# A fused attention and feed-forward kernel: second copy of the gather indices, another setup, other places for late weight splits

## The reference

```
q, k, v = x Wq', x Wk', x Wv'          (32 query heads, 8 key heads, 128 wide)
q, k    = rope(rmsnorm(q)), rope(rmsnorm(k))
keys    = [512 cached keys read by page number, 128 new keys]
p       = softmax(q keys' / sqrt(128), cached keys beyond the length hidden)
c       = (p values) Wo'               (batch b reads 16 pages named by an index input)
s       = silu(c Wgate'), the smaller half of each row by magnitude set to 0
h       = s * (c Wup');  x1 = h Wdown' + x
y       = x1 weight[adapter of b]';  out = x1 + bias + (y W4')      (W4 unpacked from 4 bits)
```

## Time and profile before

| | us |
|---|---|
| three timed runs | 1416.01, 1419.3, 1423.49 |
| median | 1419.3 |
| profiled execution, device time | 1421.85 |
| its span, first to last instruction | 1419.8 |

### The profile page before, as it was taken

How to read it: one execution, slowest core, us unless ns; L and a number is a source line. 1 busy time by engine, 2 the same in 40 slices (tenths; PEclk the granted TensorE clock), 3 DMA queues, 4 the chain that set the end, 5 groups by cost and what they waited for, 6 DMA issues and landing times.

```text
span 1419.8 us, 22844 instructions
## 1 busy us (share of the span) xinstructions
PE 1374.2 (97%) x7750; PEld 1158.6 (82%) x7750; DVE 1186.1 (84%) x2596; ACT 876.2 (62%) x2228; POOL 786.7 (55%) x822
## 2 busy tenths in 40 slices
PE   5899999999999999999999999999999999999998
PEld 4788888888888888888878888888888777676766
DVE  7989898989898989898979898989899987666662
ACT  5667676767676767676757676767677752322221
POOL 6666666666666666666566656665766620222211
PEclk9999999999999999999999999999999999999999
DMA  6110211121111112111211121111121203121121
GB/s 222 60 31 27 75 61 34 34 72 60 30 58 48 60 31 75 32 61 33 71 30 60 33 73 33 62 33 66 37 71 31 102 19 117 48 73 45 45 62 51
DMA packets 26768, 80.41 MB, mean 57 GB/s; under 512 B 9523, under 2 KB 10547, under 8 KB 23187
## 3 DMA queue, kind: packets, MB, share of 16 engines
q1 hardware_dynamic: 10258, 45.29, 9.0%
q0 software_dynamic: 16384, 33.59, 8.1%
HBM read 76.74 MB, written 2.10 MB: 56 GB/s over the span
## 4 chain that ended last, share of the span: by engine, by line
PE 72%; POOL 9%; issue 7%; DVE 6%; DMA 4%; ACT 1%; SPq 0%; another core or an unknown queue 0%; POOLq 0%; DVEq 0%; ACTq 0%
PE proj_ps L108 7%; PE proj_ps L110 7%; PE turn_ps L715 7%; PE proj_ps L109 7%; PE out_ps L894 5%; PE value_ps L108 4%; POOL kg L515 4%; PE score_ps L110 4%; PE value_ps L109 4%; PE value_ps L110 4%; PE score_ps L108 4%; PE score_ps L109 3%; DMA vg<-vc,idx 3%; PE gu_ps L110 3%; PE gu_ps L108 3%
## 5 line engine op out<-in xcount | busy, mean ns | idle before, releaser
L515 POOL DMA_INDIRECT kg<-kc,idx x256 | 258.8, 1011 | 262.9 <-issue 257.0
L1129 ACT ACTIVATE probs<-probs,shift,rstd 128x640 f32<-128x640 f32 x256 | 234.4, 918 | 157.8 <-DVE shift L1441 154.0
L525 POOL DMA_INDIRECT vg<-vc,idx x256 | 258.6, 1010 | 71.4 <-issue 70.5
L1477 DVE TENSOR_TENSOR pt_lo<-turn_ps,pt_hi 128x512 fp32r<-128x512 f32 x320 | 217.4, 687 | 47.5 <-ACT pt_hi L1135 32.1
L1452 DVE CUSTOM_DVE_ANT_0 probs<-score_ps,mask 128x640 f32<-128x640 f32 x256 | 208.4, 820 | 42.6 <-PE score_ps L110 39.7
L1135 ACT ACTIVATE pt_hi<-turn_ps 128x512 fp32r<-128x512 f32 x320 | 186.7, 593 | 88.1 <-PE turn_ps L715 78.7
L108 PE MATMUL proj_ps<-w_hi,xt_hi 128*128 128x512 f32 (+1 forms) x512 | 196.3, 383 | 13.6 <-DVE w_lo L1373 9.7
L715 PE MATMUL turn_ps<-cst,probs 128*128 128x128 f32 x1280 | 192.1, 272 | 2.7 <-DVE qt_lo L1429 2.7
L715 PEld LDWEIGHTS turn_ps<-cst,probs 128*128 128x128 f32 x1280 | 157.6, 141 | 29.0 <-issue 1.8
L110 PE MATMUL proj_ps<-w_hi,xt_lo 128*128 128x512 f32 (+1 forms) x512 | 174.7, 341 | 0.0
L109 PE MATMUL proj_ps<-w_lo,xt_hi 128*128 128x512 f32 (+1 forms) x512 | 174.1, 340 | 0.0
(11 more groups left out here) (196 smaller groups left out, 3189.9 us busy)
## 6 DMA issues: line engine op xcount, KB each, us to landing
w_raw<-wqkv SPq DMA_DIRECT2D x7, 1536.0 KB, 6.5
wo_raw<-wo SPq DMA_DIRECT2D x8, 1024.0 KB
wa_sb<-wa SPq DMA_DIRECT2D x7, 1024.0 KB, 4.8
kg<-kc,idx POOLq DMA_INDIRECT x256
vg<-vc,idx POOLq DMA_INDIRECT x256
wg_raw<-wg SPq DMA_DIRECT2D x2, 1376.0 KB, 6.2
wu_raw<-wu SPq DMA_DIRECT2D x1, 2752.0 KB
wd_sb<-wd SPq DMA_DIRECT2D x1, 2560.0 KB, 9.9
```

Source lines behind the costliest of these rows:

```text
L515: pool.indirect_dma_start(kg[:, b % 2, c, :], None, kc, bass.IndirectOffsetOnAxis(ap=idx[:, b * NC + c:b * NC + c + 1], axis=0))\
L525: pool.indirect_dma_start(vg[:, b % 2, c, :], None, vc, bass.IndirectOffsetOnAxis(ap=idx[:, b * NC + c:b * NC + c + 1], axis=0))\
L1129: act.activation(row, row, ACT.Exp, bias=shift[:, h:h + 1], scale=rstd[:, b % 2, h:h + 1], accum_out=sums[:, h:h + 1])\
L1477: dve.tensor_tensor(pt_lo[:, at, :], turn_ps[1 - j % 2][:, :], pt_hi[:, at, :].bitcast(F32), ALU.subtract).then_inc(p_lo_done[j], 1)
```

## The change

- `idx` has two copies. The numbers of head g are written to copy g % 2 from the other one, and the wait is for the transfers of the head before the last.
- x is laid out by batch: hi and lo part of one batch stand side by side (`xt_parts`), so the places of the first batches are free for gate weights earlier. `WG_HI_AT` and `WG_LO_AT` give the steps of the gate splits: ACT at 54, 56, 57, 58, DVE at 55, 57, 58, 59, 60.
- Setup has an order of its own on PE and ACT (`steps_ahead`) instead of steps -3 to -1. PE starts with six products of zeros. The k and v of the first three steps are projected into `value_ps`, so that they need not wait for `proj_ps` to be read. The masks move from DVE to ACT (a Relu, with the sign turned, and `maxima` subtracts), three of the six `tables` that DVE made move to POOL (`signed_weights` once, then two `table` instructions for each), and `split_wo` of head 0 moves into step 0.
- All four lo parts of the up weights are made on DVE, in the first late step, and `up` of batch 0 waits for each piece by itself.

```diff
-WU_ON_DVE = (2, 3)
-WG_AT = {STEPS - 7: 0, STEPS - 6: 3, STEPS - 5: 1, STEPS - 4: 2}
+WG_HI_AT = {STEPS - 10: 0, STEPS - 8: 1, STEPS - 7: 2, STEPS - 6: 3}
+WG_LO_AT = {STEPS - 9: (0, 1), STEPS - 7: (2, None), STEPS - 6: (3, 4), STEPS - 5: (5, None), STEPS - 4: (6, 7)}
-WG_FREE = {0: STEPS - 4, 3: STEPS - 4, 1: STEPS - 1, 2: STEPS}
+WG_FREE = (STEPS - 6, STEPS - 4, STEPS - 3, STEPS - 2)
+FILLED = 6
+            def kv_ps(s):
+                return value_ps if s < FIRST else proj_ps
+            xt_parts = sb("xt_parts", [P, B, 2, NK, S], F32R)
+            x_places = nc.alloc_sbuf_tensor_at("x_places", [P, B, 2, NK, S], F32, offset=xt_at)
+            xt_hi, xt_lo, x_raw = xt_parts[:, :, 0], xt_parts[:, :, 1], x_places[:, :, 1]
-            idx = sb("idx", [P, B * NC], U32)
+            idx = sb("idx", [P, 2, B * NC], U32)
...
                         if b == 0 and g > 0:
-                            hold([(place, s // 2 * (NC * 16)) for place in k_in + v_in])
-                            pool.tensor_scalar(idx[:, :], idx[:, :], 1.0, None, ALU.add).then_inc(idx_ready, 1)
+                            hold([(place, (s - B) // 2 * (NC * 16)) for place in k_in + v_in])
+                            pool.tensor_scalar(idx[:, g % 2, :], idx[:, (g - 1) % 2, :], 1.0, None, ALU.add)\
+                                .then_inc(idx_ready, 1)
...
                             gather_k(s + 3, b3, g + (b + 3) // B)
+                        if s < 4:
+                            table(s // 2, 2, s % 2)
...
+                    def signed_weights():
+                        lo, hi = slice(0, D // 2), slice(D // 2, D)
+                        pool.wait_ge(table_in, 2 * 16)
+                        for n, factor in enumerate((1.0, float(D) ** 0.5)):
+                            pool.tensor_scalar(signed[:, n, 0, :], qkw[:, n, :], factor, None, ALU.mult)
+                            pool.tensor_scalar(signed[:, n, 1, lo], qkw[:, n, hi], -factor, None, ALU.mult)
+                            pool.tensor_scalar(signed[:, n, 1, hi], qkw[:, n, lo], factor, None, ALU.mult)\
+                                .then_inc(signed_done, 1)
...
+                        pool.tensor_tensor(
+                            to[:, bs, :].rearrange("p b (h f) -> p b h f", h=2),
+                            (cosines, sines)[part][:, bs, :].unsqueeze(2).broadcast_to(shape),
+                            signed[:, n, part, :].rearrange("p (h f) -> p h f", h=2).unsqueeze(1).broadcast_to(shape),
+                            ALU.mult).then_inc(pool_tables_done[n], 1)
...
-                        if s == STEPS - 3:
-                            for k in range(NK):
-                                if k not in WU_ON_DVE:
-                                    split_up(pool, k)
...
                         if j == 0:
                             wait(pe, v_lo_done, s + 1)
+                            if s == 0:
+                                wait(pe, kv_copied, FIRST)
...
-                            wait(pe, wu_lo_done, NK)
+                        if i == 0 and bank == 0:
+                            wait(pe, wu_lo_done, ks[-1] + 1)
...
+                        pe.wait_ge(filled, 1)
+                        for _ in range(FILLED):
+                            pe.matmul(value_ps[:, :], probs[:, 0, 0, 0:P], probs[:, 0, 0, 0:DM], start=True, stop=True)
+                        pe.wait_ge(const_in, 2 * 16)
+                        for ks in ((0, 1), (2,), (3,)):
+                            project_q(0, 0, 0, ks)
+                        project_kv(0, 0, 0, range(NK))
+                        for ks in ((0, 1), (2,), (3,)):
+                            project_q(1, 1, 0, ks)
+                        turn_cached_k(0, 0)
+                        turn_q(0, 0)
+                        project_kv(1, 1, 0, range(NK))
+                        project_q(2, 2, 0, (0, 1))
+                        turn_new_k(0)
...
+                        scores(0, (0, 1))
+                        project_kv(2, 2, 0, range(NK))
+                        scores(0, (2, 3))
...
+                        turn_probs(0, 0, 0)
+                        scores(1, (2, 3))
...
+                    def hide_keys(b):
+                        act.wait_ge(key_in, 16)
+                        act.activation(mask[:, b, 0:L], key_no, ACT.Relu, bias=hide_from[:, b:b + 1], scale=HIDE)\
+                            .then_inc(mask_done, 1)
...
+                        exps(0, 0, (3,))
+                        copy_kv(2, 2)
+                        split_v(0, 0)
+                        squares(2)
+                        split_probs(0, 0, 0)
+                        exps(1, 1, (0,))
+                        hide_keys(2)
+                        split_x(4)
+                        hide_keys(3)
...
-                                1.0, -3e38, ALU.add, ALU.max, row_max[:, h:h + 1]).then_inc(max_done[h], 1)
+                                1.0, -3e38, ALU.subtract, ALU.max, row_max[:, h:h + 1]).then_inc(max_done[h], 1)
...
                     def first_late_step(s, b):
                         split_probs(s, b, 1)
                         split_probs(s, b, 2)
-                        normalise(s + 1, b + 1, (0,))
+                        normalise(s + 1, b + 1, (0, 1))
                         split_probs(s, b, 3)
-                        normalise(s + 1, b + 1, (1,))
+                        split_up(0)
                         split_probs(s, b, 4)
+                        split_up(1)
                         normalise(s + 1, b + 1, (2, 3))
                         split_o(s)
-                        for k in WU_ON_DVE:
-                            split_up(dve, k)
+                        split_up(2)
+                        split_up(3)
```

More of the change, by code:

```diff
@@ L147, in adaln_attn_ffn @@
         tables_done = [semaphore(f"tables_done{n}") for n in range(2)]
+        pool_tables_done = [semaphore(f"pool_tables_done{n}") for n in range(2)]
+        filled = semaphore("filled")
+        signed_done = semaphore("signed_done")
         mask_done = semaphore("mask_done")
@@ L665, in project_kv @@
                                 wait(pe, w_lo_done[2], g + 1)
-                            wait(pe, q_copied, s + 1)
+                            if s < FIRST:
+                                wait(pe, kv_copied, s)
+                            else:
+                                wait(pe, q_copied, s + 1)
                         for k in ks:
-                            last = product3(pe, proj_ps[:, 0:2 * D], (xt_hi[:, b, k, :], xt_lo[:, b, k, :]),
+                            last = product3(pe, kv_ps(s)[:, 0:2 * D], (xt_hi[:, b, k, :], xt_lo[:, b, k, :]),
                                             (w_hi[:, k, GQ:GW], w_lo[:, k, GQ:GW]), k == 0, k == NK - 1)
```

174 lines of the change are left out of this document (104 added, 70 removed).

## The result

The changed kernel takes 1399.2 us (median of 4 runs, 1398.2 to 1399.7), the kernel before beside it 1418.4 (4 runs, 1416.0 to 1423.5). The ratio is 0.986, with a 95% interval of 0.983 to 0.989: faster by 1.4%, some 19 us. The forecast was 1392, its range 1384 to 1403, so the direction was right, the time is in that range, and 7 us of the expected gain did not come. It lies outside the 1387 to 1397 that the forecast's own case had.

The account below looks back on a forecast made before the run. PE was taken as the bound, busy 1374 of 1419.8 us, so gains come from its stands and low clock. Terms 18.1 + 6.1 + 3 + 2 = 29.2 off 1421.85 gave 1392 us, range 1384 to 1403.

Parts of the forecast that it names:

- the forecast's own case: Whole kernel: all four terms come as summed, 1392 us, its own range 1387 to 1397, chance 0.58.
- the first rival: After setup: POOL or ACT is late, so the setup's gain goes and the time is 1398 us; chance 0.16.
- the 6.1: Setup's net gain in us: step 0 starting 8.5 earlier, less a 2.4 wait of PE in step 0.
- all cover holds: Whole kernel: setup gives 9, steps 4.5 and last steps 3.9 us, so 1385 us; chance 0.06.
- Indices, 18.1: Seven index steps: POOL's wait for gathers goes, winning 11.9 of waits, 3.5 beside them and 2.7 of low clock.
- The start of step 0, 8.5 earlier: Setup: the new order walked by durations puts step 0 at 38.6 us instead of 47.13.
- the case that I gave 0.06: Setup and steps 0 to 3: POOL's new operations hold up DVE, 4.5 us lost, 1396.5 us; chance 0.06.
- 2.4 given back: Step 0: ACT's added masks, x and wo_hi work delays the second turned probabilities, so PE waits 2.4 us.
- my theory of the clock: Setup, steps 0 and 1: low clock, with POOL's hold on DVE, cost the 4.3 us beyond forecast; stated for the experiments.
- Steps 1 to 5, 3: Steps 1 to 5: DVE loses masks and tables to ACT and POOL, winning 3 us, bounds 0 and 4.5.
- last steps, 2: Feed-forward change: wu_lo moved to DVE and earlier gate pieces shorten PE's waits, 2.0 us, bounds -1 and 3.9.
- The subtracting maximum: DVE's maxima: subtracting costs more than 0.82 us each, as two passes 1480 us, making the kernel slower; chance 0.02.

Follow-up runs that it names:

- the edit alone: Kernel before with only the gather indices kept in two halves, so the next head's are written while this head's last gathers run: 1403.9 us, ratio 0.989.
- the tables on DVE: Changed kernel with ACT's and POOL's new orders, key tables of batches 3 to 5 on DVE: 1398.4 us; with POOL's small multiplications and remaining tables last: 1398.8.
- ACT's order: Changed kernel with key hiding, x (4) and wo splits moved behind step 1's exponentials on ACT in step 0: 1397.4 us, ratio 0.984.
- POOL's: Changed kernel with POOL computing the norms of batch 2 ahead of the low parts of the values of step 0: 1397.8 us, ratio 0.984.
- both orders: Changed kernel with ACT's exponentials moved ahead in step 0 and POOL's norms of batch 2 ahead of step 0's low value parts: 1397.4 us, ratio 0.984.

## Why the forecast was right, and where it was not

- **The total.** The forecast's own case ends at 1397, and 1399.2 is nearest to the 1398 of the first rival, the case in which setup gains nothing in the end. That did come, nearly: 1.8 us of the 6.1 are left. But it came by another way than through POOL. (The case in which all cover holds adds up to 1386, not 1385.)
- **Indices, 18.1.** The mechanism holds, and by PE's starts the seven steps gave 16.4. The term that was too large is the 0.5 us that each wait should cost beside itself, 3.5 in all, read from the times of two additions. By PE's starts a step with a wait of 1.74 took 19.13, 2.00 more than the 17.13 of its neighbours, so it was 0.26, 1.8 in all. The low clock of the 23.5 us step cost the 2.7 that I had. And I took nothing for the other steps, where 1.1 comes back in the changed kernel, none of it with the edit alone. Net 15.3.
- **The start of step 0, 8.5 earlier.** It came 6.7 earlier. Up to the scores of step 0 the walk was right: q of step 0 done at 13.4 (forecast 14.5, since the zeros run longer and the first products are not at half clock), the scores end at 28.7 (29.1). The last links were too short, by two things of the same size. The normalisation took 3.18 and not 2.03: the case that I gave 0.06, a POOL operation that holds up DVE, stood here, and without it or with it moved the first turned probabilities come 0.6 and 1.1 us earlier. And the 16 instructions ahead of step 0 took 3.80 us at half clock where they take 2.60 at full, 1.2 more, which my chain had left out. The clock fell there behind a stand of 2.04 ahead of the turn of `rot_k`; in four variants that have the same stand it did not fall.
- **2.4 given back.** The hole is there, 2.43, at its place and with its cause: ACT's masks, x and both `wo_hi` end at 42.9, and the exponential follows. But steps 0 and 1 lost 4.9. Step 0 lost 4.2: the hole, and 1.75 us by which PE is busy longer, with 3.4 us at half clock behind the hole. Step 1 lost 0.7 in waits. I had counted one wait, and neither the clock behind it nor the sum of DVE's work. In the kernel before DVE is busy for 32.4 of 35.2 us there; after, for 35.8 of 40.0, from two tables (1.5 us), a third addition of a rotation (0.7), and 1.6 us in which POOL holds up `wo_lo` and a shift:

```profile
47.13:82.28 35.15, 34.88 (x210) 30.29 (x208) 32.38 (x75) 25.22 (x68) 25.14 (x26) 1.00 0.19 61
```

```profile
40.43:80.47 40.04, 36.71 (x210) 31.38 (x208) 35.77 (x80) 27.82 (x71) 31.29 (x35) 0.96 0.17 55
```

  The first is the kernel before, the second after. So my theory of the clock holds ahead of step 0, where it is worth 1.2, and falls in steps 0 and 1: with the clock full throughout they take 39.9 to 41.5 us in four variants, and 39.7 to 41.4 in the others with this setup. In two of these four DVE was busy for 99.7% of step 0 (20.34 of 20.41 and 21.72 of 21.79), so there DVE took the clock's place as what bounds the step, in part with time in which POOL holds it up; in the other two, with the tables on DVE, it was busy for 93 and 94%. In the changed kernel itself DVE is idle for 2.9 of the 21.4 us of step 0. And with DVE's tables added and POOL's hold smaller, DVE was busy for 37.0 us instead of 38.9, and the two steps took 0.6 more, not less, with a wait of 2.2 for POOL's `v_lo`. No run took work from DVE alone there. So which wait must go for these steps to be shorter stays open.
- **Steps 1 to 5, 3; last steps, 2.** 2.2 by PE's starts (2.9 by the additions, which the forecast went by), and 2.1. Both are within what was forecast. Of the pieces of the latter, the waits of 1.6 and 1.2 became 0.2 and 0.9, 1.7 in all.
- **POOL late after setup.** It did not come in the changed kernel: its six multiplications took 3.2 us (forecast 2.1), its gathers started at 47.0 (45.0), and no wait for `v_lo` of step 1 stands in the trace, since PE was later too. In four variants that made PE earlier (ACT's order, POOL's, both, and both with the tables), this wait was there, 0.3 to 2.2 us.
- **The subtracting maximum** takes 0.82 as before; that rival is out.
- The Trainium skill, SBUF — State Buffer, section "SBUF: two separate sides", on the exclusive pair of ports of DVE and GpSimd, agrees with 3.18 against 2.14, with 2.51 against 0.69, and with a shift of 2.55 instead of 0.15. I named it and gave the case that follows from it too small a chance.

The lowest medians are those of the changed kernel with ACT's other order and of both orders, 1397.4. Against the changed kernel that is 0.1%, less than these runs tell apart.

## What to carry over

Work that is moved out of a prologue has to be added up over the steps that receive it, for each engine, not only looked for in the next wait: here 6.7 us won before step 0 became 1.8 two steps later. When two profiles are compared, look first where TensorE's clock was low in each; in six variants here 1.2 us of the gain ahead of step 0 was the clock. Subtract at the starts of the engine that must not stand; those of another engine shift the cost between steps, by 1 us in 16 here. Before an operation of GpSimd on SBUF tiles is set beside VectorE's, look which VectorE operations fall into its time; 1 us of the one can cost the other 1 us. And a buffer kept twice was worth more than all the rest together, since its wait came back once per head.

## What was not expected of the hardware

- A plain float32 product of 128 x 512 stands in the trace as two instructions: six of them are twelve instructions in 7.59 us, the clock full only for the last 3.2. With the 0.44 of the earlier trace rows for one instruction, such a product is 0.88 us at full clock, four times a rounded one (0.23 from one to the next). I had taken half of that.
- GpSimd's multiplication of 128 x 64 to 128 x 128 by a constant takes 0.37 to 0.66 us. The shortest are 0.37 for 64 columns and 0.53 for 128, so a part of it does not grow with the columns.
- In two variants an ACT copy began over 3 us after the product that it waits for (3.03 and 3.64 us with no engine named), and PE then waited 3.9 and 1.7 us. It was not in the kernels before and after at these places. What delays it is open.
- The hold between DVE and GpSimd goes both ways: GpSimd's product of 384 columns, begun while DVE's subtraction of 1024 ran, took 1.98 us instead of 1.08.
